# A fused attention and expert layer on one core: first tile table ahead of batch 2's residual, statistics of batches 5 to 7 inside the tile loop, third expert weight behind the first tiles' rows

## The reference

```python
x = x + _layernorm(_L0_attn_ref(_layernorm(x), W_in, b_in, W_out, b_out, decay, mix))
x = x + _layernorm(_L0_ffn_ref(_layernorm(x), gate_kernel, w0, w1, wo))

# attention: inp = mix * x + (1 - mix) * x shifted by one token
#            h = relu(inp @ W_in.T + b_in);  state = state * decay + h (a scan over tokens)
#            out = state @ W_out.T + b_out
# experts:   8 experts, the best 2 of each token by x @ gate_kernel, softmax of those two;
#            y = (silu(t @ w0[e]) * (t @ w1[e])) @ wo[e]   with w0, w1: 128 x 512, wo: 512 x 128
```

## Time and profile before

| | us |
|---|---|
| three runs | 271.58, 270.92, 273.17 (median 271.58) |
| profiled execution, device time | 271.02 |
| its span from first to last instruction | 269.2 |
| PE busy | 242.1 (90% of the span) |
| DVE busy | 184.7 (69%) |
| ACT busy | 180.0 (67%) |
| POOL busy | 167.3 (62%) |

### The profile page before, as it was taken

How to read it: one execution, slowest core, us unless ns; L and a number is a source line. 1 busy time by engine, 2 the same in 40 slices (tenths; PEclk the granted TensorE clock), 3 DMA queues, 4 the chain that set the end, 5 groups by cost and what they waited for, 6 DMA issues and landing times.

```text
span 269.2 us, 8125 instructions
## 1 busy us (share of the span) xinstructions
PE 242.1 (90%) x2071; PEld 230.2 (86%) x2071; DVE 184.7 (69%) x811; ACT 180.0 (67%) x521; POOL 167.3 (62%) x190
## 2 busy tenths in 40 slices
PE   6977847899999999999999999999999999999800
PEld 2745726899999999999999999999999999999700
DVE  4678997877756876776678677843434334998754
ACT  3176775677778768696776678656566565668592
POOL 3317773786787878877788877775324233277740
PEclk9999995999999999999999999999999999999965
DMA  6999972313421321331132123323232209302048
GB/s 172 289 322 369 358 222 54 81 41 84 121 70 43 99 73 39 84 92 51 45 89 82 42 71 92 110 87 95 75 92 56 62 19 358 159 18 97 13 152 234
DMA packets 29676, 31.70 MB, mean 118 GB/s; under 512 B 4779, under 2 KB 22189, under 8 KB 29505
## 3 DMA queue, kind: packets, MB, share of 16 engines
q1 hardware_dynamic: 24448, 22.56, 27.8%
q0 software_dynamic: 4320, 8.50, 9.1%
q10 hardware_dynamic: 864, 0.13, 0.3%
HBM read 19.58 MB, written 12.05 MB: 117 GB/s over the span
## 4 chain that ended last, share of the span: by engine, by line
PE 79%; DVE 11%; DMA 3%; issue 2%; ACT 2%; DVEq 1%; SPq 0%; POOL 0%; POOLq 0%
PE bank L1763 47%; PE bank L1800 24%; PE bank L1758 3%; PE bank L1714 2%; DVE sb_early L1002 2%; DMA sb_gate_w<-in_L_ffn_gate_kernel 1%; DMA sb_early<-pair_rows 1%; PE bank L1664 1%; DVE sb_x L1017 1%; DVE sb_stats L948 1%; DVE sb_rest_stats L978 1%; PE bank L1682 1%; DMA pair_rows<-sb_y_rows,sb_y_pair 1%; PE bank L1690 1%; ACT sb_square L647 1%
## 5 line engine op out<-in xcount | busy, mean ns | idle before, releaser
L1763 PE MATMUL bank<-sb_xeT,sb_w_now 128*128 128x128 f32 x1136 | 140.5, 277 | 0.0
L1763 PEld LDWEIGHTS bank<-sb_xeT,sb_w_now 128*128 128x128 f32 x1136 | 134.4, 194 | 0.5 <-issue 0.3
L527 POOL DMA_INDIRECT pair_rows<-sb_y_rows,sb_y_pair x71 | 74.6, 1050 | 51.3 <-ACT sb_y_rows L771 30.3
L1369 DVE TENSOR_TENSOR sb_gated<-bank,sb_silu 128x512 f32<-128x512 f32 x71 | 48.9, 689 | 59.1 <-PE bank L1763 51.6
L514 POOL DMA_INDIRECT expert_rows<-sb_row,sb_place x64 | 64.4, 1006 | 30.1 <-issue 16.4
L1800 PE MATMUL bank<-sb_w_raw,sb_gated 128*128 x568 | 75.4, 276 | 0.1
L1800 PEld LDWEIGHTS bank<-sb_w_raw,sb_gated 128*128 128x128 f32 x568 | 69.1, 192 | 0.3 <-issue 0.2
L742 ACT ACTIVATE sb_silu<-bank 128x512 f32<-128x512 f32 x71 | 42.3, 595 | 17.4 <-PE bank L1763 17.4
L737 ACT ACTIVATE sb_xeT<-bank 128x128 f32<-128x128 f32 x71 | 19.5, 274 | 44.4 <-PE bank L1758 43.5
L760 ACT ACTIVATE sb_w_now<-sb_w_raw 128x512 f32 x71 | 44.3, 624 | 0.4 <-issue 0.4
L1388 DVE COPY sb_w_now<-sb_w_raw 128x512 f32 x71 | 30.1, 424 | 1.4 <-issue 1.4
(11 more groups left out here) (204 smaller groups left out, 252.5 us busy)
## 6 DMA issues: line engine op xcount, KB each, us to landing
sb_taken_rows<-expert_rows SPq DMA_DIRECT2D x71, 65.5 KB, 1.9
sb_w_raw<-in_L_ffn_w SPq DMA_DIRECT2D x2, 2048.0 KB, 16.4
sb_pairs_early<-pair_rows SPq DMA_DIRECT2D x3, 1024.0 KB, 6.9
out_dram<-sb_x SPq DMA_DIRECT2D x3, 512.0 KB, 3.2
pair_rows<-sb_y_rows,sb_y_pair POOLq DMA_INDIRECT x71, 2.3
sb_x<-in_L_attn_x SPq DMA_DIRECT2D x4, 256.0 KB, 4.1
sb_pairs_early<-in_x_turned SPq DMA_DIRECT2D x4, 256.0 KB, 4.5
sb_pairs_early<-in_x_turned SPq DMA_DIRECT2D x1, 1024.0 KB, 8.0
```

The costliest lines, as they stand in the source:

```text
L527: pool.indirect_dma_start(pair_rows[:, :], bass.IndirectOffsetOnAxis(ap=y_pair[group % 2][:, t % PAIRS:t % PAIRS + 1], axis=0), y_rows[slo ...
L1369: dve.tensor_tensor(gated[t % 2][:], p_l2[:], silu[t % 2][:], ALU.mult).then_inc(c["gated"], 1)
L1763: last = pe.matmul(to[:, n * P:(n + 1) * P], w[:, n * P:(n + 1) * P], x, start=True, stop=True)
```

## The change

On **DVE** the four sums of batch 4 go in three pieces into places further ahead. The statistics of batches 5 to 7 leave the list before the loop; four groups of three sums go behind the gate and weight copy of slots 3 to 6, and the twelve aggregates into slot 7. Table 0 then comes ahead of the residual of batch 2, and `use_tiles(0)` behind it. The scan of batch 3 moves from slot 0 to a place ahead of `choose(2)`, the weight copy of tile 1 ahead of `put(2)`, and the offset and tags of batch 2 from the head of slot 0 to the end of slot 1; `use_tiles(1)` goes there too, and `table_start(2)` to slot 2. On **ACT** the root for batches 5 to 7 falls away, the Silu table is loaded after `relu(3)`, the squares of batch 2 come behind `first_part(0)`, and its normalised rows in slots 1 and 2 instead of 0 and 1. On **POOL** a new step `rest_power` (an add and a power over 12 columns) takes the place of ACT's root and DVE's reciprocal, behind `send_y(3)` in slot 7. On **PE** the ranks of batch 2 and the attention output of batch 3 come behind w0 and w1 of tile 0, and the fills are counted anew. On **SP** the load of wo is issued behind the loads of tiles 0 to 2.

```diff
+REST_SUMS = ((0, 3), (3, 6), (6, 9), (9, 12))
@@ sync
             load_w(1, w1_in)
-            sp.dma_start(w_raw[:, 2 * WCOLS:]...).then_inc(s_w_in[2], 16)
+            def load_wo():
+                sp.dma_start(w_raw[:, 2 * WCOLS:]...).then_inc(s_w_in[2], 16)
...
                     load_tile(t, row_of_first if t == first_tile(p) else first_row(t))
+                if p == 0:
+                    load_wo()
@@ gpsimd
+            def rest_power():
+                pool.wait_ge(rest["mv"], 1)
+                pool.tensor_tensor(rest_sd[:], rest_mv[:, :, 1],
+                                   eps[:].broadcast_to([P, (B - REST) * G]),
+                                   ALU.add).then_inc(rest["sd"], 1)
+                pool.wait_ge(rest["sd"], 1)
+                pool.tensor_tensor(rest_rs[:], rest_sd[:],
+                                   minus_half[:].broadcast_to([P, (B - REST) * G]),
+                                   ALU.pow).then_inc(rest["rs"], 1)
             for k, s, t in slots():
                 a_slot(k, s, t)
                 send_y(t - 4)
+                if t == 3 + len(REST_SUMS):
+                    rest_power()
@@ scalar
             root2(2)
-            rest_root()
-            act.activation(unused[:], eps[:], ACT.Silu)
             keep_z(6)
             keep_z(7)
             relu(3)
+            act.activation(unused[:], eps[:], ACT.Silu)
             chunk_of(0)
             fetch_w0(0)
-            squares(2, 0, G)
             for k, s, t in slots():
                 first_part(t)
+                if t == 0:
+                    squares(2, 0, G)
...
-                if t < 2:
-                    normalise3(2, G // 2 * t, G // 2 * (t + 1))
+                if t in (1, 2):
+                    normalise3(2, G // 2 * (t - 1), G // 2 * t)
@@ vector (sums1 now takes a range; pieces (0, 1), (1, 2), (2, G) of batch 4 stand further ahead)
             scan(2)
             scale_z(3)
-            start1(4)
-            rest_sums(0, (B - REST) * G)
-            rest_mean_var()
-            inverse(1, 4, REST, sd1, rs1)
+            mean_var(1, 4, mv1, stats1)
             table_start(0)
             table_end(0)
+            residual(2)
             use_tiles(0)
-            residual(2)
             top(2)
             choice(2)
+            chunk_of(0)
+            chunk_of(1)
+            fetch_w1(0)
+            scan(3)
             choose(2)
-            rest_inverse()
-            chunk_of(0)
-            fetch_w1(0)
-            put(2)
+            inverse(1, 4, REST, sd1, rs1)
             table_start(1)
             table_end(1)
-            use_tiles(1)
+            fetch_w1(1)
+            put(2)
...
                 pairs_of_tiles(t)
+                if t == 1:
+                    offset3(2)
+                    tags(2)
+                    use_tiles(1)
+                elif t == 2:
+                    table_start(2)
+                elif 3 <= t < 3 + len(REST_SUMS):
+                    rest_sums(*REST_SUMS[t - 3])
+                elif t == 3 + len(REST_SUMS):
+                    rest_mean_var(0, (B - REST) * G)
@@ tensor
-            pe.wait_ge(a["z_kept"], B - 3)
-            fill(p_l1, 7)
-            ranks(2)
+            pe.wait_ge(a["count"], 2)
+            fill(p_choice, 10)
...
                 if t == 0:
-                    fill(p_l1, 2)
-                two_layers(t - 1)
+                    fill(p_l1, 1)
+                elif t == 1:
+                    two_layers(0)
+                    ranks(2)
+                    times_w_out(3)
+                if t > 1:
+                    two_layers(t - 1)
```

More of the change, by code:

```diff
@@ L361, in _ @@
             load_w(1, w1_in)
-            sp.dma_start(w_raw[:, 2 * WCOLS:].rearrange("p (e c n) -> p e c n", e=E, c=FC),
-                         wo_in.rearrange("e (c p) n -> p e c n", p=P)).then_inc(s_w_in[2], 16)
+            def load_wo():
+                sp.dma_start(w_raw[:, 2 * WCOLS:].rearrange("p (e c n) -> p e c n", e=E, c=FC),
+                             wo_in.rearrange("e (c p) n -> p e c n", p=P)).then_inc(s_w_in[2], 16)
             def first_row(t):
@@ L624, in mean_of_x @@
                                scale=-D ** -0.5).then_inc(a["mean1"], 1)
-            def rest_root():
-                act.wait_ge(rest["mv"], 1)
-                act.activation(rest_sd[:], rest_mv[:, :, 1], ACT.Sqrt,
-                               bias=eps[:]).then_inc(rest["sd"], 1)
             def rest_means():
@@ L943, in inverse, with sums1 @@
                     dve.wait_ge(a[f"late_rs{k}"], b - root_last + 1)
-            def sums1(b):
-                dve.wait_ge(s_x[min(b, X_LOADS - 1)], 16)
-                for j in range(G):
+            def sums1(b, first=0, end=G):
+                if first == 0:
+                    dve.wait_ge(s_x[min(b, X_LOADS - 1)], 16)
+                for j in range(first, end):
                     last = dve.bn_stats(stats1[b][:, j, :], x_tile(b, j))
-                last.then_inc(a["stats1"], 1)
+                if end == G:
+                    last.then_inc(a["stats1"], 1)
             def scale_half(b, h):
@@ L980, in rest_sums, with rest_mean_var @@
                     last.then_inc(rest["stats"], 1)
-            def rest_mean_var():
-                dve.wait_ge(rest["stats"], 1)
-                for n in range((B - REST) * G):
+            def rest_mean_var(first, end):
+                if first == 0:
+                    dve.wait_ge(rest["stats"], 1)
+                for n in range(first, end):
                     last = dve.bn_aggr(rest_mv[:, n, :], rest_stats[:, n, :])
-                last.then_inc(rest["mv"], 1)
-            def rest_inverse():
-                dve.wait_ge(rest["sd"], 1)
-                dve.reciprocal(rest_rs[:], rest_sd[:]).then_inc(rest["rs"], 1)
+                if end == (B - REST) * G:
+                    last.then_inc(rest["mv"], 1)
             def mix_rows(b):
@@ L1359, in a_slot @@
                 else:
-                    if to_scan is not None:
+                    if to_scan is not None and to_scan > FIRST_IN_SLOTS:
                         scan(to_scan)
@@ L1519, in _ @@
             offset3(0)
+            sums1(4, 0, 1)
             put(0)
@@ L1525, in _ @@
             scale_z(2)
+            sums1(4, 1, 2)
             residual(1)
@@ L1529, in _ @@
             choose(1)
+            sums1(4, 2, G)
             offset3(1)
@@ L1566, in _ @@
                     a_slot(t, 0)
-                chunk_of(t + 1)
-                times_gate_curve(t - 1)
-                fetch_w1(t + 1)
+                if t > 0:
+                    chunk_of(t + 1)
+                    times_gate_curve(t - 1)
+                    fetch_w1(t + 1)
                 pairs_of_tiles(t)
+                if t == 1:
[8 more added lines that the diff above has]
+                    rest_mean_var(0, (B - REST) * G)
                 if k in ROUNDS:
@@ L1746, in a_slot @@
                 if part == 0:
-                    if to_w_out is not None:
+                    if to_w_out is not None and to_w_out > FIRST_IN_SLOTS:
                         times_w_out(to_w_out)
```

7 lines of the change are left out of this document (1 added, 6 removed).

## The result

The changed kernel takes 275.1 us (median of four runs, 274.7 to 276.02), the kernel before 271.28 in the same comparison; the ratio is 1.0131 with a 95% interval of 1.0075 to 1.0187. The forecast was 273.0 with a range up to 274.9: slower was right, the size was not. The profiled execution took 274.71 us with a span of 273.0, 3.8 longer than before, where 1.5 was forecast. Over all comparisons nearly every run of the kernel before lies near 271 us or near 272.8, so 1.5 us between two single executions need not come from an edit.

A forecast was written before the change was run, and what follows sets the result against it. PE was taken as full with POOL right behind: batch 3's sends 3.35 us later, less 1.0 returned, 2.35, less slack 0.86, gave 1.5; 271.0 + 1.5 = 272.5, against the median 273.0, range 269.6 to 274.9.

The forecast's parts named there:

- The early start: Before the tile loop: table 0 at 31.7, tile 0 loaded near 35.4, batch 2's offset on DVE 0.8 us earlier.
- The third weight: Load of wo: issued near 38, landed near 46.2, costing nothing by itself unless later than 50.97.
- The residual of batch 3: On DVE: starts at 55.55 instead of 56.76, 1.2 us earlier; bound 56.76, no gain.
- The statistics: Batches 5 to 7: 12.7 us to the variances at 68.25, power 2.3, batch 3's sends at 71.15, 3.35 later.
- Rival 1: POOL's power step costs nothing, only slot 5 limits: 1.6 us gain, 270.0; chance 0.15.
- The return of 1.0 us: On POOL: y(4), sent behind DVE's scan and no longer held by it, gives back 1.0 us of 1.96.
- Rival 4: y(4) is not held by the scan, so nothing returns: 274.0; chance 0.14.
- The slack in slot 13: 0.86 us between y(9) leaving its bank and wo of tile 11 on PE, absorbing part of the 2.35 delay.
- The sum: PE 1.5 us later from slot 13 on, staying 1.5: 272.5, against the median 273.1, said as 273.0.
- The likeliest case: Whole kernel: a time between 268.9 and 274.3, within one per cent (2.7 us) of before; chance 0.68.
- a rival of its own: Third weight lands after 50.97, holding tile 3 and slots 2 and 3; at 55 costs 4.0, 275.6; chance 0.05.

The follow-up runs named there:

- 3: The changed kernel with the third weight in two halves, behind the second weight and behind the loads of tiles 0 to 2: 274.26 us, ratio 1.0108.
- 1: The changed kernel with the third weight issued in its old place, right behind the second weight: 277.01 us, ratio 1.0216.
- 6: The changed kernel with the third weight back in front and batch 2's squares, ranks, offset and tags ahead of tile 0's work again: 273.98 us, ratio 1.009.
- 2: The changed kernel with the sums and aggregates of batches 5 to 7 in slot 2 and POOL's power in slot 6, ahead of y(3): 271.88 us, ratio 1.0007.
- 7: As 6, but sums of batches 5 to 7 in slots 1 to 4, aggregates in slot 5, POOL's power in slot 6: 271.58 us, ratio 1.001.
- 4: The changed kernel with POOL's power over 12 columns made twice, the first into an unread buffer: 279.59 us, ratio 1.0298.
- 11: As 2, statistics of batches 5 to 7 in slot 2, but POOL's power back in slot 7 ahead of batch 3's sends: 272.29 us, ratio 1.0019.

## Why the prediction was right in direction and short in size

**The early start.** Table 0 at 31.52 (forecast 31.7), the load of tile 0 at 35.27 (35.4), the offset of batch 2 0.8 us earlier (0.8): right. That POOL lets only a little of it through was right too: with tile 0 4.4 us ahead, the first send of batch 2 is 0.8 ahead (forecast 1.2).

**The third weight: the term that was mis-sized first.** 6.5 us at 322 GB/s and 1.7 for landing gave 46.2; it took 11.0 from issue, to 49.1. Near that rate the DMA engines moved data from 40 to 46 only (300 GB/s), with 139 ahead and 152 behind: a slow start and a tail for which the term had no room. And nothing was charged for batch 1's last sends, which land behind the weight and put the load of tile 3 at 48.03. The prediction set aside a weight later than 46.2 but under 50.97 as free "by itself". It was not: with tile 3 and the half clock it took the lead of 4.4 us to a lag of 0.8 by slot 5. The rule of the Trainium skill that was cited (DMA: Bandwidth & Descriptors, Queues, rings and completion order: the descriptors of one queue are taken in ring order on each engine) doesn't reach this case: the sends go through another queue, and the trace shows them held all the same.

**The residual of batch 3: the step that failed.** 55.55 was forecast, with 56.76 (no gain) as the bound; it came at 57.14, outside the bound. 3 puts at least half of these 1.6 us down to the weight (56.33 there, with the rows of tile 3 still late). The rest is the changed order itself, as 1 and 6 show: batch 2 hangs behind tile 0, and DVE has more to do ahead of the residual.

**The statistics: right, and the main cause.** From 57.14 the stretch up to the variances took 12.7 us, as forecast (the last aggregate ends at 69.83), the power 2.32 (2.3), and the sends of batch 3 came 1.55 later than forecast because the residual did. 2 and 7 take the step out of the way and win back 3.0 and 3.3 us by the spans (7 against 6; by the medians 2.4); 4 doubles it and PE pays in full; 11 parts it into wait and work. Rival 1, that the power step costs nothing, falls.

**The return of 1.0 us: right.** y(4) took 1.00 behind the scan, 1.00 in 11, and 1.85 in 7, where it starts 0.2 us into the scan and ends 0.8 after it, as in rows 3 and 4. Rival 4 falls. The Trainium skill (SBUF — State Buffer, Who interferes with whom) infers that an instruction with two SBUF inputs leaves the writing of descriptors alone, and says that it contends with a GpSimd instruction that reads SBUF. A send also reads the places of its rows (`sb_place`, `sb_y_pair`), and no run parts the reading from the writing, so the hold is shown, and which of the two is held is open.

**The slack in slot 13: mis-sized.** 0.86 was read from y(9) and wo of tile 11. What ends last is the gate of tile 11, which stands on DVE behind the residual and which PE needs for w1 of tile 12. The deviation of batch 4 came 3.85 us late (84.45 against 80.60), wo of tile 11 3.38: the slack is 0.47.

**The sum.** 2.3 us are missing: 1.5 from the residual, 0.4 from the slack, 0.4 in slots 16 and 17, for which the forecast had nothing ("Later phases repeat these steps with POOL no further behind, so it stays 1.5"). There the same chain acts once more: DVE waits 0.64 us for POOL's second deviation of batch 4 (93.74; before, at 89.72, it had no wait), and the gate of tile 14 behind it comes at 94.98 instead of 90.97, 4.0 later where wo of tile 13 is 3.4 later. That is read from the trace; no run was aimed at it. The likeliest case had been a change of under one per cent, at 0.68; the ratio of 1.013 fell into the 0.23 for slower, and the median lies 0.2 above the range, whose upper end held the loss for a late weight only as a rival of its own and not on top of the forecast.

## What to carry to other kernels

A wait put into an engine's queue costs what is queued behind it: before a step is moved to POOL or DVE, list the next five instructions there and who waits for them, and put the step where that engine idles anyway (2.6 us of POOL and a wait for late sums cost 3 us ahead of batch 3's sends, and left PE without a wait in slot 13 ahead of y(3)). An early start is worth only what the slowest chain behind it lets through, and parts that are made to depend on one early load (three engines on tile 0's rows here) lose together when it is late. Charge a big transfer not only for its own landing but for every small one that lands behind it.
